# Starting the wide block's network inside its attention, and another order of the second experts' first steps

## Chip, cores and metric

The kernel runs on one core of a Trainium2 chip. The metric is the time of one execution in microseconds on the device, the median of several runs.

## What is computed

Four transformer blocks, each an attention and a network, on 1024 tokens (8 tiles of 128) of width 128. All is fp32. The change touches the second block, here called the wide block, and its experts:

```python
x = x + _L1_xattn_ref(_layernorm(x, axis=-1), ctx_1024, ...)
x = x + _L1_ffn_ref(_layernorm(x, axis=-1), ...)

# _L1_xattn_ref, 16 heads of width 128 and one score of a token with itself
x1 = _layernorm(attn_out + state_seq, g1, b1)
mlp = jax.nn.relu(x1 @ Wg + bg) * (x1 @ Wl + bl) @ Wm + bm      # width 512
return _layernorm(mlp + x1, g2, b2)

# _L1_ffn_ref, 16 experts of width 256, the best 2 of each token
logits = jnp.einsum('sbd,de->sbe', x, Wg) + bg + bias
vals, idx = jax.lax.top_k(logits, TOP_K)
w = jax.nn.softmax(vals - jnp.max(vals, axis=-1, keepdims=True), axis=-1)
cw = jnp.einsum('sbk,sbke->sbe', w, jax.nn.one_hot(idx, NUM_EXPERTS, dtype=x.dtype))
h = jax.nn.relu(jnp.einsum('sbd,edh->esbh', x, W1) + b1[:, None, None, :])
y = jnp.einsum('esbh,ehd->esbd', h, W2) + b2[:, None, None, :]
out = jnp.einsum('esbd,sbe->sbd', y, cw)
```

## The kernel before

Five engines each run one fixed list of instructions, in order, and meet at semaphores. Tokens are handled in two halves of 512. PSUM has 8 banks of 128x512. Products that need fp32 accuracy on the fast path are split in a high and a low part: `split_products` issues three 128x512 matmuls (low by high, high by low, high by high).

**Attention of the wide block.** `pipelined` writes out 32 steps (16 heads by 2 halves of tokens) of many stages. An entry `(stage, positions, lag)` runs the stage's unit n in step n + lag, in the order of the list. The stages `output` (lag 6) and `turn_sums` (lag 7) end it: the last heads' product is summed in bank 6, ScalarE copies it (`copy_sums`), TensorE turns it into bank 3, VectorE adds it to the tokens (`residual`, which counts `y_read`). The first half's norm is made in between (`statistics`, `variance`, `centre`, `scale`), so its tokens are turned in step 34 (`enter_mlp`), copied by ScalarE (`enter_halves`: the rounded `in_hi` and the full `xnT`) and their low part made by VectorE (`split_input(0)`).

**The wide block's network** (`ffn(mlp1)`). Per half: four slices `fc` of the hidden layer, each a gate product and an up product (3 matmuls each), ScalarE's relu, VectorE's `gate`, then `output`, 32 instructions of 128 columns. The second half's norm stands in VectorE's list ahead of the first gates (`mlp_norm(1)`). With 3 gate banks, slice 3 waits for the gate of slice 0 (`h_ready`).

**The experts** (`mixed(ffn1)`). 32 steps, each one expert and one half, in the list `order`; `hidden(s)` is 2 slices of 3 matmuls. The first 6 steps are *plain*: `plain_output` multiplies with fp32 weights and VectorE adds the result to the tokens by the routing weight `cw`. From step 6 on, VectorE scales the hidden layer itself by `cw_wide`, a row of routing weights spread over all partitions, and ScalarE and GpSimd split the result. `cw_wide` comes by a detour: TensorE turns `cw` (`turn_weights`), ScalarE copies it (`copy_weights`), SyncE stores it to DRAM (`cw_rows`) and loads two rows spread out (`load_wide`, 512 KB each). In TensorE's list of before: turn half 0, `hidden(0)`, turn half 1, `hidden(1)`, `routing`, `hidden(2)`, `plain_output(0)`, `hidden(3)`, `plain_output(1)`, `turn_weights`, `hidden(4)`, `plain_output(2)`, and so on.

**Weights.** An expert's first weights go through one staging buffer `w_in` (128 KB a load, `load_first`), the second ones through `w_out[e % 2]` (`load_second`). For experts 0 and 1 GpSimd makes both parts (`split_weights`); from expert 2 on ScalarE makes the high part (`round_first(e)`, which waits for the load) and GpSimd the low part (`split_first`), which then frees `w_in` for the next load. All loads are in SyncE's one list: `load_first(2)`, `load_first(3)`, `load_second(2)`, the store and two `load_wide`, `load_second(3)` (which waits for the second plain output of expert 1), `load_first(4)`, ... ScalarE's list has `router_exp` (the exponential that routing needs) at the start of step 2, `round_first(2)` after step 2, `round_first(3)` after step 3, then `copy_weights`, and `round_first(4)` after step 5.

`keep_busy(bank, n)` issues 2n matmul instructions of 128 columns with no use, so that TensorE is not idle. `inverse_roots` is GpSimd's part of a norm.

## Time and profile before

| | us |
|---|---|
| median of 3 runs | 779.91 (774.3 to 782.99) |
| the profiled execution's own time | 780.78 |
| its span, first to last instruction | 779.1 |
| TensorE busy | 723.9 (93%) |
| VectorE, ScalarE, GpSimd busy | 520.3, 458.7, 419.5 |
| mean granted TensorE clock, of full speed | 0.985 |

The wide block's attention lies at about 185 to 358 us, its network at 358 to 385, the experts' plain steps at 385 to 422. Matmuls are pipelined: a 128x512 one shows a duration of 0.39 us and starts 0.23 us after the one before.

### The profile page before, as it was taken

To read this page: it belongs to the slowest core of one execution; us is meant where nothing else is said; L and a number is where in the kernel's file an instruction comes from. 1 tells how busy PE (TensorE), PEld (TensorE's weight loads), DVE (VectorE), ACT (ScalarE), POOL (GpSimd) and SP (SyncE) were. 2 spreads that over 40 slices of the span, in tenths; PEclk is the share of its full clock that TensorE was granted. 3 is DMA by queue.
4 is the path that set the end of the run, shared out by engine and by line. 5 is a ranking of instruction groups with operands and counts; after the bars stand their busy time and mean duration, and the time that the engine had idled before them with its cause. 6 is when DMAs were issued, how large, how long until landed. Compare 5 with 4: busy or idle time off the path is not lost. (4 is left out here: it accounts for less than half of the span.)

```text
span 779.1 us, 14669 instructions
## 1 busy us (share of the span) xinstructions
PE 723.9 (93%) x5099; PEld 586.2 (75%) x5099; DVE 520.3 (67%) x1380; ACT 458.7 (59%) x1388; POOL 419.5 (54%) x414
## 2 busy tenths in 40 slices
PE   6989999998899999898979999989889999999896
PEld 3657987776788878776878788756668888888796
DVE  6888666676766666576756676658866466656666
ACT  3993556675877777563135676469924456656322
POOL 6875157774767543433223677466342378787311
PEclk9999999999999999899999999979999999999999
DMA  8004032210000000000003345000010232210000
GB/s 292 2 2 150 1 124 88 88 55 1 2 1 2 8 1 1 1 2 1 8 29 132 122 155 167 24 2 2 2 42 28 98 106 70 74 62 1 1 1 28
DMA packets 16361, 38.47 MB, mean 49 GB/s; under 512 B 1896, under 2 KB 6272, under 8 KB 16032
## 3 DMA queue, kind: packets, MB, share of 16 engines
q1 hardware_dynamic: 16288, 37.53, 14.3%
q8 instruction: 41, 0.67, 0.3%
q14 instruction: 32, 0.26, 0.1%
HBM read 36.87 MB, written 0.66 MB: 48 GB/s over the span
## 5 line engine op out<-in xcount | busy, mean ns | idle before, releaser
L1347 PE MATMUL banks<-input_hi,weights_in_lo 128*128 128x512 f32 x296 | 120.4, 407 | 5.2 <-PEq L1748 3.0
L1347 PE MATMUL banks<-input_lo,weights_in_hi 128*128 128x512 f32 x296 | 115.9, 391 | 0.0
L1347 PE MATMUL banks<-input_hi,weights_in_hi 128*128 128x512 f32 x296 | 115.7, 391 | 0.0
L1058 ACT ACTIVATE probabilities<-banks,neg_max 128x128 f32<-128x128 f32 x256 | 91.1, 470 | 12.6 <-DVE neg_max L2116 12.6
L877 POOL TENSOR_TENSOR hidden_lo<-hidden,hidden_hi 128x512 fp32r<-128x512 f32 x50 | 64.5, 1295 | 38.2 <-ACT hidden L1217 34.9
L725 POOL TENSOR_TENSOR rstd<-var_eps,neg_half 128x4 f32<-128x4 f32 x23 | 23.7, 1032 | 98.2 <-POOLq L724 78.6
L1058 ACT ACTIVATION_READ_ACCUMULATOR probabilities<-banks,neg_max 128x1 f32 x256 | 73.2, 311 | 0.0
L884 POOL TENSOR_TENSOR hidden<-hidden,scratch 128x512 f32<-128x512 f32 x48 | 62.1, 1293 | 19.7 <-ACT hidden L1203 17.2
L1347 PEld LDWEIGHTS banks<-input_hi,weights_in_lo 128*128 128x128 f32 x296 | 55.8, 189 | 19.6 <-issue 4.4
L1347 PE MATMUL banks<-hidden_hi,weights_out_lo 128*128 128x512 f32 x164 | 67.9, 414 | 1.5 <-POOL weights_out_lo L867 1.2
L1203 ACT ACTIVATE hidden<-banks 128x512 f32<-128x512 f32 x64 | 38.2, 598 | 51.8 <-PE banks L1347 51.6
L834 POOL TENSOR_TENSOR weights_in_lo<-weights_in,weights_in_hi 128x256 fp32r<-128x256 f32 (+2 forms) x31 | 40.1, 1293 | 52.6 <-ACT weights_in_hi L1228 51.7
L935 POOL TENSOR_TENSOR scratch<-values_state,self_weight 128x512 f32<-128x512 f32 x32 | 33.3, 1040 | 60.0 <-DVE self_weight L2275 60.0
L1347 PE MATMUL banks<-hidden_hi,weights_out_hi 128*128 128x512 f32 x164 | 65.2, 398 | 0.0
L1347 PEld LDWEIGHTS banks<-input_hi,weights_in_hi 128*128 128x128 f32 x296 | 55.6, 188 | 12.3
L1347 PEld LDWEIGHTS banks<-input_lo,weights_in_hi 128*128 128x128 f32 x296 | 55.9, 189 | 10.1
L1347 PE MATMUL banks<-weights_out,hidden 128*128 128x128 f32 x480 | 57.0, 276 | 2.5 <-PEq L1698 1.8
L1347 PEld LDWEIGHTS banks<-weights_out,hidden 128*128 128x128 f32 x480 | 55.7, 192 | 4.1 <-issue 2.3
L2464 DVE TENSOR_TENSOR banks<-banks,hidden 128x512 f32<-128x512 f32 x48 | 33.5, 698 | 33.1 <-POOL hidden L884 32.6
L2258 DVE TENSOR_REDUCE row_max<-banks 128x4 f32<-128x512 f32 x32 | 22.1, 691 | 47.1 <-PE banks L1593 47.1
L1347 PEld LDWEIGHTS banks<-identity 128*128 128x128 f32 x380 | 47.4, 197 | 7.3 <-issue 4.1
L1347 PE MATMUL banks<-identity 128*128 128x128 f32 x380 | 51.8, 284 | 1.0 <-DVE queries_feat L2070 1.0
(298 smaller groups left out, 1836.1 us busy)
## 6 DMA issues: line engine op xcount, KB each, us to landing
scratch<-cw_rows SPq DMA_DIRECT2D x25, 512.0 KB, 3.8
weights_out<-w_in SPq DMA_DIRECT2D x17, 256.0 KB, 2.8
weights_in<-w_in SPq DMA_DIRECT2D x8, 512.0 KB, 3.7
weights_in<-w_in SPq DMA_DIRECT2D x9, 256.0 KB, 2.7
weights_in<-w_in SPq DMA_DIRECT2D x16, 128.0 KB, 2.2
weights_out<-w_in SPq DMA_DIRECT2D x16, 128.0 KB, 2.1
wq<-w_in SPq DMA_DIRECT2D x1, 1024.0 KB, 5.2
wo<-w_in SPq DMA_DIRECT2D x1, 1024.0 KB, 7.4
```

Source lines behind the costliest of these rows:

```text
L725: pool.tensor_tensor(rstd[:, four], var_eps[:, four], neg_half[:, four], ALU.pow)\
L834: return pool.tensor_tensor(lo, raw, hi, ALU.subtract)
L877: pool.tensor_tensor(h_lo[:, j, :], h_full[:, j, :], h_hi32[:, j, :], ALU.subtract)\
L884: pool.tensor_tensor(h, h, cw_wide[:, e % 2, half * 512:(half + 1) * 512], ALU.mult)\
L935: pool.tensor_tensor(mva[:, n % 2, :, :], mv[:, four, :], self_w[:, n % 2, :, None].broadcast_to([P, 4, D]), ALU.mult)\
L1058: act.activation(prob[:, n // 2 % 2, h, :], b8(n % (2 if prune else 3))[:, i, :], ACT.Exp, bias=neg_max8[:, n % 4, i:i + 1], accum_out=z[: ...
L1203: act.activation(h_full[:, j, :], bank[f.hidden_bank(s, fc)][:, :], f.first, **kw)\
L1347: return pe.matmul(o, l, rh, start=start, stop=stop, **kw)
L2258: dve.tensor_reduce(m, b4(1 + n % 2), X_AX, ALU.max, negate=True).then_inc(st.sem, st.one())
L2464: dve.tensor_tensor(up, up, h, ALU.mult).then_inc(weighted_ready, 1)
```

## The change

Four things.

1. **Gates in the attention.** TensorE's gate products of slices 0 and 1, half 0, move from `ffn(mlp1)` into step 36 of the attention's list (`first_gates`), ahead of the last head's output. The up products get banks 5, 4, 3, so only slice 2 still waits for `y_read`. VectorE makes `split_input(0)` in step 35. The second half's norm is dealt out between the gates of the first half.
2. **Attention's first steps.** Turning the second half of the tokens, its copies and its keys and values (`turn_state`, `state_rest`, `take_tokens`, `evacuate_state_keys`, `state_values`) move one step later.
3. **Experts' order.** Steps 0 to 3 are now (expert 0, half 0), (1, 0), (0, 1), (1, 1). TensorE's list: turn half 0, filler, `hidden(0)`, `hidden(1)`, `plain_output(0)`, `plain_output(1)`, filler of 28 instructions, turn half 1, `routing`, small filler, `hidden(2)` to `hidden(5)`, `turn_weights`, `plain_output(2)`, `plain_output(3)`, and from `hidden(6)` on as before.
4. **Around it.** GpSimd splits expert 0's and expert 1's weights earlier in its list. ScalarE copies `xnT` ahead of `in_hi`; `router_exp` moves to the start of step 4, behind `round_first(3)`; `copy_weights` to step 5. SyncE's `load_second(2)` moves behind the two `load_wide`.

```diff
@@ class FFN
-                return 7 if self.gated and self.E == 1 else self.output_bank(half)
+                return 7 if self.gated and self.E == 1 else 4 + 3 * half if self.FC == 2 else self.output_bank(half)
+            def up_bank(self, fc):
+                return 5 - fc % 3
@@ class Experts
-                if gamma:
+                if gamma or self.FC == 2:
                     self.order[0:4] = [(0, 0), (1, 0), (0, 1), (1, 1)]
-                return (1, 0)
+                return (2, 0) if self.FC == 2 else (1, 0)
@@ SyncE, load_mixed
+                if f.gated:
                     load_second(2)
...
                 if f.gamma:
                     load_first(3)
+                if not f.gated:
                     load_second(2)
@@ GpSimd
-            inverse_roots((0, 0, 1))
+            inverse_roots((0,))
             split_weights(ffn1, 0)
-            inverse_roots((1,))
+            inverse_roots((0,))
+            split_weights(ffn1, 1)
+            inverse_roots((1, 1))
             mixed(ffn1)
@@ ScalarE, mixed
-                    if s == 2:
+                    if s == (4 if f.FC == 2 else 2):
                         router_exp()
...
                     if s in (2, 3):
                         round_first(s)
+                    if s == (5 if f.FC == 2 else f.turn_at):
+                        copy_weights()
                     if s == 5:
                         round_first(4)
-                    if s == f.turn_at:
-                        copy_weights()
@@ TensorE, wide_attention
+                def first_gates(it, n):
+                    pe.wait_ge(w_in_ready[0], 1)
+                    pe.sem_inc(w_in_ready[0], -1)
+                    pe.wait_ge(input_ready, 1)
+                    pe.sem_inc(input_ready, -1)
+                    mlp_gate(0, 0)
+                    mlp_gate(0, 1)
...
-                               (scores, range(32), 0), (state_rest, (0,), 1), (enter_mlp, (0,), 34)],
+                               (scores, range(32), 0), (state_rest, (0,), 2), (enter_mlp, (0,), 34),
+                               (first_gates, (0,), 36)],
@@ TensorE, ffn
-                                keep_busy(6, 5)
+                                keep_busy(6, 3)
                             pe.wait_ge(h_ready, 1)
...
-                            if half == 0 and fc == 0:
+                            if half == 0 and fc == 2:
                                 pe.wait_ge(y_read, 2)
@@ TensorE, mixed
-                    if s == 0 and not f.gated and not f.gamma:
+                    if s == 0 and f.FC == 2:
                         transpose_half(0, source, f.entry_bank(0))
-                    if s == 1 and not f.gamma:
-                        if not f.gated:
-                            keep_busy(6, 8)
+                        keep_busy(6, 12)
+                    if s == 2 and f.FC == 2:
+                        keep_busy(4, 14)
                         transpose_half(1, source, f.entry_bank(1))
-                    if s < 2 and not f.gamma:
-                        keep_busy(0 if f.gated and s == 0 else 6, ((16, 7), (3, 9))[f.gated][s])
+                        routing()
+                        keep_busy(0, 2)
...
-                    elif s == 1:
+                    elif s == 1 and f.gated:
                         routing()
...
-                    if f.lag <= s < f.lag + f.plain:
+                    if f.FC == 2 and s == 5:
+                        turn_weights()
+                    if f.FC == 2 and s < f.lag + 4:
+                        for step in {1: (0, 1), 5: (2, 3)}.get(s, ()):
+                            plain_output(step)
+                    elif f.lag <= s < f.lag + f.plain:
                         plain_output(s - f.lag)
...
-                    if s == f.turn_at and not f.gated and not f.gamma:
-                        turn_weights()
@@ VectorE, ffn
-                    for fc in range(f.FC):
-                        gate(0, fc)
+                    norm_stats(1, att, 1e-6)
+                    gate(0, 0)
+                    gate(0, 1)
+                    norm_apply(1, att, xm, norm_tok_ready, "g1", lambda b: row("be1"), lambda: gate(0, 2))
+                    dve.sem_inc(rows_wanted, 1)
+                    gate(0, 3)
                     split_input(1)
```

## Rows read from the trace of the kernel before

**Rows 1.** Waits of TensorE, 340 to 430 us.

```profile
PE banks L1358 <- PEq L1356: 2.0, 1, 2.0
```

**Rows 2.** Timeline of TensorE (start, length, instruction, [idle before]), attention's end.

```profile
356.26 0.50 PE L1347 MATMUL banks<-hidden_hi,hidden_lo 128*128 128x512 f32 x1 [0.72 <-DVE hidden_lo L2251]
...
357.92 0.66 PE L1644 MATMUL banks<-identity,scratch 128*128 128x128 f32 x4 [0.69 <-ACT scratch L1138]
...
366.80 1.06 PE L1347 MATMUL banks<-identity 128*128 128x128 f32 x8
...
368.53 3.70 PE L1347 MATMUL banks<-weights_out,hidden 128*128 128x128 f32 x31 [0.68 <-PEq L1698]
```

**Rows 3.** Timeline of VectorE, norms of the wide block.

```profile
378.37 1.13 DVE L2038 SCALAR_TENSOR_TENSOR x_tok<-values_state,rstd,x_tok 128x128 f32<-128x128 f32 x4
...
389.44 1.62 DVE L2038 SCALAR_TENSOR_TENSOR x_tok<-values_state,rstd,x_tok 128x128 f32<-128x128 f32 x4 [0.17 <-DVEq L2035]
```

**Rows 4.** Timeline of GpSimd: splitting expert 0's first weights.

```profile
389.40 0.72 POOL L834 TENSOR_TENSOR weights_in_lo<-weights_in,weights_in_hi 128x256 fp32r<-128x256 f32 x1
```

**Rows 5.** Timeline of TensorE, the experts' first steps.

```profile
385.00 3.74 PE L1347 MATMUL banks<-identity 128*128 128x128 f32 x32
...
390.47 0.47 PE L1347 MATMUL banks<-input_hi,weights_in_lo 128*128 128x512 f32 x1 [1.73 <-PEq L1748]
...
391.92 1.95 PE L1347 MATMUL banks<-identity 128*128 128x128 f32 x16
...
400.19 1.85 PE L1347 MATMUL banks<-square_weights,xn_feat 128*128 128x16 f32 x16
...
408.87 1.03 PE L1794 MATMUL banks<-identity,combine_weights 128*16 128x128 f32 x8 [0.41 <-PEq L1789]
...
423.65 0.50 PE L1347 MATMUL banks<-input_hi,weights_in_lo 128*128 128x512 f32 x1 [0.36 <-DVE hidden_lo L2481]
```

**Rows 6.** Timeline of ScalarE, experts' first steps; last row from block 0.

```profile
399.70 1.38 ACT L1203 ACTIVATE hidden<-banks,cols 128x512 f32<-128x512 f32 x2 [2.00 <-PE banks L1347]
...
404.37 0.21 ACT L1164 ACTIVATE gap_exp<-gap 128x8 f32<-128x8 f32 x1 [3.30 <-ACTq L1163]
...
405.63 0.41 ACT L1228 ACTIVATE weights_in_hi<-weights_in 128x256 fp32r<-128x256 f32 x1
...
409.36 0.42 ACT L1228 ACTIVATE weights_in_hi<-weights_in 128x256 fp32r<-128x256 f32 x1 [1.96 <-ACTq L1222]
...
420.48 0.42 ACT L1228 ACTIVATE weights_in_hi<-weights_in 128x256 fp32r<-128x256 f32 x1 [5.23 <-ACTq L1222]
...
106.44 0.72 ACT L1225 ACTIVATE weights_in_hi<-weights_in,cols 128x512 fp32r<-128x512 f32 x1 [5.54 <-ACTq L1222]
```

**Rows 7.** Timeline of VectorE, routing.

```profile
404.02 0.17 DVE L2353 TENSOR_TENSOR gap<-best 128x8 f32<-128x8 f32 x1
...
408.22 0.29 DVE L2382 TENSOR_TENSOR combine_weights<-combine_weights,combine_weights_second 128x128 f32<-128x128 f32 x1
```

**Rows 8.** Timeline of the DMA queue (start of issue); last two rows from block 0.

```profile
412.74 0.80 SPq L631 DMA_DIRECT2D scratch<-cw_rows  x2
...
416.76 0.33 SPq L612 DMA_DIRECT2D weights_in<-w_in  x1
...
100.50 0.80 SPq L631 DMA_DIRECT2D scratch<-cw_rows  x2
...
101.41 0.36 SPq L612 DMA_DIRECT2D weights_in<-w_in  x1
```

**Rows 9.** Timeline of TensorE: its two longest waits.

```profile
316.57 0.65 PE L1347 MATMUL banks<-scratch,ones 128*32 128x128 f32 x8 [2.88 <-POOL scratch L927]
...
577.75 0.63 PE L1358 MATMUL banks<-identity,xn_tok 128*128 128x128 f32 x4 [2.42 <-PEq L1356]
```

**Rows 10.** Windows of 4 us; the granted clock is third from the end.

```profile
316.00:320.00 4.00, 3.43 (x18) 2.68 (x19) 0.88 (x6) 1.16 (x3) 2.74 (x3) 0.50 0.01 4
...
320.00:324.00 4.00, 4.00 (x23) 3.77 (x22) 3.48 (x13) 1.82 (x9) 0.30 (x1) 0.65 0.00 0
```

More of the change, by code:

```diff
@@ L885, in scale @@
                         .then_inc(scaled_ready, 1)
-                if not f.gamma:
+                if f.gated:
                     split_weights(f, 1)
@@ L1027, in take @@
                     source = bank[f.entry_bank(half)][:, :]
+                    act.activation(xnT[:, tokens], source, ACT.Copy).then_inc(feat_ready, 1)
                     act.activation(in_hi[:, 0, tokens], source, ACT.Copy).then_inc(st.sem, st.one())
-                    act.activation(xnT[:, tokens], source, ACT.Copy).then_inc(st.sem, st.one())
                     act.wait_ge(st.sem, st.n)
                     act.sem_inc(input_hi_ready, 1)
-                    act.sem_inc(feat_ready, 1)
                 if not begun:
@@ L1100, in evacuate_state_keys @@
                 act.wait_ge(projected_act, half + 3)
-                act.activation(qT[:, half * 512:(half + 1) * 512], bank[2 + half][:, :], ACT.Identity,
+                act.activation(qT[:, half * 512:(half + 1) * 512], bank[2 + 4 * half][:, :], ACT.Identity,
                                bias=col("bk1")).then_inc(keys_ready, 1)
@@ L1151, in enter_mlp @@
                     enter_halves(mlp1)
-                pipelined(act, [(take_tokens, (1,), 0), (enter_mlp, (0,), 35),
+                pipelined(act, [(enter_mlp, (0,), 35),
                                 (copy_probsT, range(32), 3), (exps, range(32), 2), (copy_own, range(32), 1),
-                                (queries, range(32), 0), (evacuate_state_keys, (1,), 0),
+                                (queries, range(32), 0), (take_tokens, (1,), 0), (evacuate_state_keys, (1,), 1),
                                 (lambda it, n: round_heads(wo1, wo_hi, 0), (2,), 0),
@@ L1575, in state_rest @@
                     pe.sem_inc(feat_ready, -1)
[L1576 removed]
+                    project(w("wk1"), xnT, 5, (1,), projected_act)
                     project_tok(w("wv1"), xnT, 4, (0,))
@@ L1649, in enter_mlp, with mlp_gate @@
                     transpose_half(0, iv, mlp1.entry_bank(0))
-                pipelined(pe, [(queries, range(32), 0), (turn_state, (0,), 0), (own_sums, range(32), 1),
+                def first_gates(it, n):
[5 more added lines that the diff above has]
+                    mlp_gate(0, 1)
+                pipelined(pe, [(queries, range(32), 0), (turn_state, (0,), 1), (own_sums, range(32), 1),
                                (output, range(32), 6), (turn_heads, range(32), 4), (turn_own, range(32), 1),
                                (values, range(32), 3), (turn_sums, (15, 31), 7), (turn, range(32), 2),
-                               (scores, range(32), 0), (state_rest, (0,), 1), (enter_mlp, (0,), 34)],
+                               (scores, range(32), 0), (state_rest, (0,), 2), (enter_mlp, (0,), 34),
+                               (first_gates, (0,), 36)],
                           32, 1, lambda: None)
+            def mlp_gate(half, fc):
+                tokens = slice(half * 512, (half + 1) * 512)
+                return split_products(bank[mlp1.hidden_bank(half, fc)][:, :],
+                                      lambda part: mlp1.w1((w_lo, w_hi)[part], 0, fc),
+                                      lambda part: (in_lo, in_hi)[part][:, 0, tokens], True, True)
             def route(weight, experts, src, at=7):
@@ L1663, in hidden @@
                 def hidden(half):
-                    if half == 0:
+                    if half == 0 and not f.gated:
                         pe.wait_ge(w_in_ready[0], 1)
                         pe.sem_inc(w_in_ready[0], -1)
-                    pe.wait_ge(input_ready, 1)
-                    pe.sem_inc(input_ready, -1)
+                    if half == 1 or not f.gated:
+                        pe.wait_ge(input_ready, 1)
+                        pe.sem_inc(input_ready, -1)
                     tokens = slice(half * 512, (half + 1) * 512)
@@ L1674, in hidden @@
                             if half == 0:
-                                keep_busy(6, 5)
+                                keep_busy(6, 3)
                             pe.wait_ge(h_ready, 1)
                         at_bank = f.hidden_bank(half, fc)
-                        m = split_products(bank[at_bank][:, :],
-                                           lambda part: f.w1((w_lo, w_hi)[part], 0, fc),
-                                           lambda part: (in_lo, in_hi)[part][:, 0, tokens], True, True)
+                        if not f.gated or half == 1 or fc >= 2:
+                            m = split_products(bank[at_bank][:, :],
+                                               lambda part: f.w1((w_lo, w_hi)[part], 0, fc),
+                                               lambda part: (in_lo, in_hi)[part][:, 0, tokens], True, True)
                         if f.gated:
-                            if half == 0 and fc == 0:
+                            if half == 0 and fc == 2:
                                 pe.wait_ge(y_read, 2)
-                            m = split_products(bank[3 + at_bank][:, :],
+                            m = split_products(bank[f.up_bank(fc)][:, :],
                                                lambda part: f.up((w_lo, w_hi)[part], 0, fc),
@@ L2232, in narrow_attention @@
                                     (copy_both, range(UNITS), 2), (first_output, (0,), 15)], UNITS, 1, st.close)
-            def mlp_norm(half, *args):
-                norm_half(half, att, xm, 1e-6, norm_tok_ready, "g1", lambda b: row("be1"), *args)
             def wide_attention():
@@ L2328, in wide_attention @@
                 st.close()
-                pipelined(dve, [(heads_out, range(32), 4), (weights, range(32), 3), (state_values, (0,), 2),
+                pipelined(dve, [(heads_out, range(32), 4), (weights, range(32), 3), (state_values, (0,), 3),
+                                (lambda it, n: split_input(0), (0,), 35),
                                 (maxima, range(32), 1), (low_headsT, range(32), 4), (second_tokens, (0,), 2),
                                 (residual, (15, 31), 7),
-                                (lambda it, n: split_input(0), (0,), 37),
                                 (statistics, (0, 2), 23), (variance, (0,), 26), (centre, (0, 2), 27),
@@ L2407, in gate @@
                     dve.sem_inc(g_done, -1)
-                    h, up = hT[:, half, fc, :], bank[3 + f.hidden_bank(half, fc)][:, :]
+                    h, up = hT[:, half, fc, :], bank[f.up_bank(fc)][:, :]
                     dve.scalar_tensor_tensor(h, up, col(f.up_bias, fc), h, ALU.add, ALU.mult)\
```

7 lines of the change are left out of this document (4 added, 3 removed).

## The prediction

> **What bounds the kernel now.** I read the page first: TensorE is busy 93% of the span and no other engine over 67%, so time can come only out of TensorE's waits, fillers and half-speed stretches. Between the attention's last head and step 8 of the experts the timeline shows which. Before the network's first output product stand a wait of 0.72 for the last head's low part, one of 0.69 for ScalarE's copy, a filler of 1.06 and a wait of 0.68 [rows 2]. Before the experts stand a filler of 3.74, a wait of 1.73, a filler of 1.95 [rows 5] and a wait of 2.0 for the tokens of half 1 [rows 1]. The next thing to read is what TensorE meets behind that stretch: step 8 waits 0.36 at 423.65 [rows 5], released by VectorE's low part, which follows ScalarE's rounding, and ScalarE had stood still 5.23 until the first weights of expert 4 were there, at 420.48 [rows 6]. That load had been issued at 416.76 [rows 8]. So the plain steps are bound twice, by TensorE and, almost level with it, by a chain: turned routing weights, their trip through DRAM, the load of expert 4, ScalarE, VectorE, TensorE. A gain ahead of step 8 counts only as far as this chain comes earlier too.
>
> **Part 1, the attention's start.** Turning half 1 one step later lets the first scores go about 0.9 earlier, and the state's projections then stand behind step 2. ScalarE's list (a rounding of weights, a copy, the exponentials) sets the third step as before. I take a gain of 0.4; bounds 0.9 and a loss of 0.3, since the projections need about 2.7 wherever they stand.
>
> **Part 2, gates in the attention.** Six matmuls of 0.23 each take the place of the wait of 0.72 [rows 2]: the last head's product starts at 356.75 instead of 356.26, the turned sums at 358.41 instead of 357.92. From there the two up products (1.4) and slice 2 (1.4) end at 361.8. VectorE: residual to 359.8, statistics of half 1 to 361.5, two gates of 0.7 to 363.0, centring 1.1, third gate 0.7, scaling 1.1: tokens of half 1 at 366.4. Slice 3 ends at 363.95 on TensorE, which then waits 2.4 for these tokens, where before it had them. The turning (0.45) and the filler of 8 (0.95) end at 367.9; the fourth gate is done at 367.2. The first output product starts at 367.9 against 368.53 [rows 2]: a gain of 0.6. The rows that GpSimd adds (two of 2.4 after 366.4, done at 371.2) are still ahead of VectorE's need of them at 371.9.
>
> **Part 3, the split of expert 0's weights.** It was the last thing that the wait until 390.47 was for: GpSimd ended it at 390.12 [rows 4, 5]. It moves to about 378, beside VectorE's norm of half 0. What that costs is shown by the same norm instruction, 1.13 for four alone and 1.62 beside this split [rows 3]; a loss of 0 to 0.5, which may eat the 0.6 above. I take 0.3. The Trainium skill (SBUF — State Buffer, Who interferes with whom) says that a VectorE instruction with two SBUF inputs and a reading GpSimd instruction exclude each other for a whole instruction. By it the first of the four would wait up to 1.0, the length of GpSimd's rounding, and nothing would be left of the gain; the row shows half of that.
>
> **Part 4, the experts' first steps.** Output products, 0.3 earlier, end at 384.2; turning and 24 fillers (2.8 at the rate of 3.74 for 32 [rows 5]) end at 387.5. VectorE has half 0's low part at 387.8, so `hidden(0)` starts there, 2.7 ahead of before. Expert 1's first weights: their load stands in SyncE's list behind `load_second(0)`, which waits for the network's last output of half 0 to be read (384.5); landing 2.2 later, split 1.9, so 389.1. `hidden(1)` starts at 389.3. Two plain outputs of 1.7 end at 394.1 and 28 fillers (3.3) at 397.4. GpSimd's root for half 1 now stands behind the split and comes about 1.5 later; the tokens of half 1 are there at 395.7, under that filler. Turning and ScalarE's copy take 1.4, 0.9 of it waiting; routing 1.7; filler 0.5: `hidden(2)` starts at about 401.0 (400.2 to 401.3). Before it was 401.9 (400.19 plus 16 pieces [rows 5]). From here on I count from this start, H.
>
> TensorE's four hidden steps end at H+5.6, and the next entry turns the routing weights. When are they ready? ScalarE ends step 2 at H+2.4 and rounds expert 2; round_first(3) needs GpSimd's split and a load, and started 3.73 after round_first(2) before (405.63 to 409.36 [rows 6]), hence H+6.1. `router_exp` now stands behind it: exponential ready at H+6.7. Before it ran 0.35 after its input (404.02, 404.37 [rows 6, 7]). Routing needs 2.75 more behind it (405.76 to the row at 408.22 and its end, 408.51 [rows 7]), and 0.36 to reach TensorE: turning starts at H+9.75. TensorE waits 4.1, which was 0.41 before [rows 5]. This is the wait that takes the place of those removed. Two plain outputs follow, the first held by VectorE's sum to H+10.9, the second ends at H+14.3. For `hidden(6)` that is 415.3, against 416.0.
>
> The chain: copies end 1.6 after the turning started, the store takes 2.0 (410.76 to 412.74), so the two wide loads are issued at H+13.4 against H+10.85 before [rows 8]. Behind them stand now three loads of 128 KB, the last, expert 4's, at H+15.1; before it was H+14.9. The nearest case in the trace is block 0: wide loads issued at 100.50, 256 KB right behind them, there at 106.4, 5.9 later [rows 6, 8]. With 0.13 MB more at some 270 GB/s I take 6.3: H+19.7, that is 420.7. Bounds: 5.8 (nothing for the larger volume) and 7.7 (before, from the wide issue at 412.74 to 420.48 [rows 6, 8]). Before, ScalarE had it at 420.4. From there to TensorE's wait it takes the same 3.2: 423.9 against 423.65. So everything gained ahead of step 8 is waited away there: a loss of 0.25, less the 0.4 of part 1. The Trainium skill (DMA: Bandwidth & Descriptors, Anatomy of one DMA) gives about 2.0 us a transfer plus its bytes at 436 GB/s. By that estimate the queue of 1.4 MB would be in 5.3 after the first issue, and the sum 1.0 lower; block 0 shows 5.9 for less.
>
> **The clock.** Two waits of TensorE in this trace reach 2.4 (2.88 and 2.42 [rows 9]). After the first, with TensorE busy throughout ahead of it, the granted clock was 0.50 and then 0.65 over 8 us [rows 10], the lower level of 1.2 GHz; the work from 316.57 to 323.3 took 6.7 where other steps show 3.9. The waits of 1.73 and 2.0 inside our stretch left it at full speed. The wait of 4.1 is beyond both, so I count a fall there: turning and two plain outputs at half speed end 2 later, half of it hidden, since TensorE would wait at step 8 anyway; the loads behind them come 0.6 to 1.1 later. I take 1.0.
>
> **Sum.** 780.78 (this execution's own time) - 0.4 + 0.25 + 1.0 = 781.6. The median shown is 0.9 below this execution, so I forecast 781.0, 1.1 above the median: no change that can be measured. A measurement of this kernel tells about 1%, 7.8 us, from no change; the three runs before lie 8.7 apart.
>
> **Rivals.**
> - *The clock falls at the gates too (slower).* TensorE idles 2.4 at 364 to 366.4, as long as the 2.42 of the trace that was followed by a fall. Low for 3.4 to 6.8 us, it would run filler and output product at half speed, and these lie on the path: 1.5 to 3. With the fall at the routing: 783.5. It decides from the length at which idle time costs the clock; between 2.0 (no fall) and 2.42 (a fall) the trace doesn't say, and a wait of 1.93 elsewhere, among sparse work, had one too.
> - *The late router isn't late (faster).* If the load of expert 3 or the exponential were there in time, turning would start at H+5.9, the wide loads at H+9.5, expert 4's at H+11, and step 8 would be reached about 3 earlier, with no fall: 776.5. Against it: ScalarE's list is in order, and 3.73 between the two roundings is measured.
> - *The clock holds at the routing.* Then the sum is 780.6, or 780.0 against the median; this differs from the forecast by less than the runs do.
> - *The reorder moves later stretches.* The falls at 316 and 577 need not come at the same places when all work before them is shifted; one more or one less is 3 either way.
>
> **Chances.** Forecast 0.40, both falls 0.25, clock holds 0.20, router in time 0.10, others 0.05. The range from 776 to 786 takes in the router in time, both falls with their upper bound of 3 and one fall elsewhere. Faster by over 1% 0.03, within 1% 0.91, slower by over 1% 0.06.
>
> **What would show it.** In the changed trace: two gate products of three ahead of the last head's output, and a wait of about 2.4 before half 1 of the network's tokens is turned; no wait for weights before `hidden(0)`; the exponential of routing directly behind the rounding of expert 3; a wait of about 4 before the routing weights are turned, a granted clock under 1 behind it; ScalarE waiting for expert 4's weights until 20 after `hidden(2)` began; and the steady steps from step 8 on within 1 of their place. The forecast is wrong if TensorE reaches step 8 early and finds the low part there, if TensorE's routing wait is short, or if the clock changes outside the stretch.

## The result, and the profile after

| | before | after |
|---|---|---|
| median of 20 runs, us | 779.89 (774.3 to 782.99) | 783.52 (776.87 to 787.16) |
| ratio, 95% interval | | 1.0057 (1.0037 to 1.0076) |
| profiled execution's own time, its span | 780.78, 779.1 | 786.86, 785.1 |
| mean granted clock | 0.985 | 0.979 |

The changed kernel is 0.6% slower (779.89 x 0.0057 = 4.4 by the ratio, 3.6 by the medians), which is inside the 1% that I called no change. Its profiled execution is 3.3 above its own median and before's 0.9 above its own, so of the 6.0 between the spans about 2.4 belong to the executions and not to the kernels.

The waits of TensorE, 340 to 430 us; columns: waiting line, releaser, us in total, times, longest:

```profile
PE banks L1353 <- PEq L1830: 3.2, 1, 3.2
PE banks L1821 <- PEq L1816: 3.0, 1, 3.0
...
PE banks L1364 <- PEq L1362: 2.2, 1, 2.2
```

Before, the longest wait of this stretch was 2.0 [rows 1]; now three reach 2.2 to 3.2. TensorE's timeline at the attention's end (start, length, instruction, [idle before]):

```profile
357.26 0.66 PE L1650 MATMUL banks<-identity,scratch 128*128 128x128 f32 x4 [0.69 <-ACT scratch L1144]
...
365.19 0.63 PE L1364 MATMUL banks<-identity,values_ctx 128*128 128x128 f32 x4 [2.17 <-PEq L1362]
365.65 1.56 PE L1353 MATMUL banks<-identity 128*128 128x128 f32 x8
367.01 4.90 PE L1353 MATMUL banks<-weights_out,hidden 128*128 128x128 f32 x32
```

The turned sums came at 357.92 and the output product at 368.53 [rows 2], so the product starts 1.5 earlier. But half 1's tokens are waited for 2.17, and the product, 3.70 long for 31 instructions before, takes 4.90 for 32 (3.74 in E2 below, at full clock). TensorE in the experts' first steps:

```profile
388.25 0.47 PE L1353 MATMUL banks<-input_hi,weights_in_lo 128*128 128x512 f32 x1 [0.33 <-PEq L1775]
...
399.48 1.93 PE L1353 MATMUL banks<-square_weights,xn_feat 128*128 128x16 f32 x16 [0.86 <-PEq L1809]
...
401.70 0.48 PE L1353 MATMUL banks<-input_hi,weights_in_lo 128*128 128x512 f32 x1
...
405.36 0.47 PE L1353 MATMUL banks<-input_hi,weights_in_lo 128*128 128x512 f32 x1 [0.65 <-PEq L1772]
...
411.34 1.87 PE L1821 MATMUL banks<-identity,combine_weights 128*16 128x128 f32 x8 [2.99 <-PEq L1816]
413.00 5.76 PE L1353 MATMUL banks<-weights_out,hidden 128*128 128x128 f32 x32
...
423.31 3.06 PE L1353 MATMUL banks<-weights_out,hidden 128*128 128x128 f32 x16 [3.18 <-PEq L1830]
...
430.66 0.39 PE L1353 MATMUL banks<-input_hi,weights_in_lo 128*128 128x512 f32 x1
```

The gain is still there at 388.25 (2.2 ahead of 390.47 [rows 5]). At 399.48 the routing is only 0.7 ahead of 400.19, but two plain outputs (391.31 to 394.88, 3.57), which stood behind it before, are done by then. So up to here the new order is some 4 ahead, and the loss lies all behind `hidden(2)`, which starts at 401.70. Turning the routing weights is 2.5 late against 408.87, after a wait of 2.99. At 423.31 the first output of expert 2 waits 3.18, and step 8's second slice is reached 7.0 after its time in [rows 5]. The releaser L1830 is TensorE's own sequencer; that line stands right behind `pe.wait_ge(w_out_loaded[sub], 16)`, the wait for the second weights. Who had those, by SyncE's queue (start of issue):

```profile
413.85 0.33 SPq L648 DMA_DIRECT2D cw_rows<-att_feat  x1
417.18 0.80 SPq L634 DMA_DIRECT2D scratch<-cw_rows  x2
418.03 1.09 SPq L625 DMA_DIRECT2D weights_out<-w_in  x2
419.27 0.33 SPq L615 DMA_DIRECT2D weights_in<-w_in  x1
```

At 417.18 the two wide loads, at 418.03 two loads of second weights (expert 2's and expert 3's), at 419.27 expert 4's first weights. Before, the wide loads went out at 412.74 and expert 4's at 416.76 [rows 8], and expert 2's second weights had been loaded ahead of the store. ScalarE:

```profile
407.66 0.42 ACT L1234 ACTIVATE weights_in_hi<-weights_in 128x256 fp32r<-128x256 f32 x1 [2.14 <-ACTq L1228]
407.98 0.19 ACT L1170 ACTIVATE gap_exp<-gap 128x8 f32<-128x8 f32 x1
...
423.82 0.42 ACT L1234 ACTIVATE weights_in_hi<-weights_in 128x256 fp32r<-128x256 f32 x1 [9.99 <-ACTq L1228]
```

The exponential stands directly behind the rounding of expert 3, 3.6 later than the 404.37 of [rows 6], and expert 4's weights are rounded at 423.82 instead of 420.48. VectorE's norm of half 0, beside which GpSimd now splits expert 0's weights, and the granted clock (third from the end) in windows of 4 us:

```profile
377.95 1.60 DVE L2068 SCALAR_TENSOR_TENSOR x_tok<-values_state,rstd,x_tok 128x128 f32<-128x128 f32 x4
```

```profile
316.00:320.00 4.00, 4.00 (x19) 3.51 (x16) 1.07 (x4) 1.45 (x3) 2.19 (x2) 0.50 0.02 4
...
364.00:368.00 4.00, 2.81 (x17) 2.84 (x18) 2.52 (x6) 1.09 (x2) 2.68 (x2) 0.76 0.00 0
...
368.00:372.00 4.00, 4.00 (x31) 3.96 (x30) 0.22 (x1) 0.00 (x0) 3.32 (x2) 0.82 0.00 0
...
412.00:416.00 4.00, 4.00 (x21) 3.69 (x20) 1.38 (x5) 1.17 (x2) 0.00 (x0) 0.50 0.12 19
...
416.00:420.00 4.00, 4.00 (x25) 3.54 (x24) 2.25 (x8) 0.00 (x0) 0.00 (x0) 0.84 0.48 100
...
424.00:428.00 4.00, 4.00 (x18) 3.62 (x18) 1.34 (x5) 2.17 (x5) 2.69 (x3) 0.57 0.02 4
```

The clock fell to its lower level of 1.2 GHz behind each of the three waits: in parts of 364 to 372, from the turning at 411.34 to 420, and in 424 to 428. The first row answers to [rows 10]: the fall after the wait of 2.88 in the attention is there as before.

### The profile page after: what moved, and what is told of

It is laid out like the page before. It is cut to its first block and busy times, and to the rows that moved or that the text cites. A ratio compares the mean times of both kernels' runs of the same rounds, so it can differ in the third digit from the quotient of the medians.

```text
span 785.1 us, 14642 instructions
## 1 busy us (share of the span) xinstructions
PE 726.8 (93%) x5089; PEld 588.8 (75%) x5089; DVE 518.6 (66%) x1380; ACT 458.2 (58%) x1388; POOL 419.5 (53%) x414
## 5 line engine op out<-in xcount | busy, mean ns | idle before, releaser
L1353 PE MATMUL banks<-weights_out,hidden 128*128 128x128 f32 x480 | 60.9, 288 | 5.5 <-PEq L1830 3.2
L1353 PEld LDWEIGHTS banks<-weights_out,hidden 128*128 128x128 f32 x480 | 59.6, 204 | 7.1 <-issue 5.5
```

Of the source, the lines that this page charges most:

```text
L1353: return pe.matmul(o, l, rh, start=start, stop=stop, **kw)
```

## The experiments

Each time is a median of 12 runs (9 of E12, 6 of E11), beside runs of the kernel before, which were 779.28 for E1 to E4, 779.90 for E5 to E8 and 778.81 for E9 to E12. Since each profile is one execution, I also read from each trace how long TensorE takes between fixed points: from the turned sums (357.92 before) to the first split output product of step 6 (425.59 before), 67.67 in the kernel before and 75.22 in the changed one. "Stretch" below is this difference.

**E1 and E2, the parts without the experts.** E1 is the kernel before with only the attention's first steps changed; E2 is the changed kernel with the experts' part of the diff put back (ScalarE's new order of its copies stays). Core of E1's edit; the copies, keys and values of half 1 move one step in the same way:

```diff
-                pipelined(pe, [(queries, range(32), 0), (turn_state, (0,), 0), (own_sums, range(32), 1),
+                pipelined(pe, [(queries, range(32), 0), (turn_state, (0,), 1), (own_sums, range(32), 1),
...
-                               (scores, range(32), 0), (state_rest, (0,), 1), (enter_mlp, (0,), 34)],
+                               (scores, range(32), 0), (state_rest, (0,), 2), (enter_mlp, (0,), 34)],
```

> The kernel before with the attention's first steps of the change alone (turning and projecting half 1 one step later). Theory A (the loss of the change lies in the experts' order, in two new waits of TensorE of 3.0 and 3.2 us and the half-speed stretches behind them; the attention's start is a gain): the queries at 312 us come 1.1 earlier, as they do in the changed kernel, and the time is 1 below before, ratio 0.998 to 1.000. Theory B (work that is shifted gains or loses falls of the clock elsewhere, and that is what the medians show): the stretch is 1.1 shorter but the median moves by up to 3 us either way.

> The changed kernel with the experts' order, routing, loads and GpSimd's list put back: what is left is the attention's start and the gates in the attention. Theory A: TensorE waits 2.2 for half 1's tokens of the network and the clock falls behind it in most executions; net of the 1.1 of the attention's start and 0.5 of the gates, less 1.3 for the clock, 0 to 2 us faster than before, ratio 0.997 to 1.000. Rival C (the gates are the loss, since a wait of 2.2 and half speed stand on the path that was covered before): 2 us or more slower, ratio over 1.002.

Measured: E1 776.98, ratio 0.9971 (0.9944 to 0.9998); E2 776.44, ratio 0.9977 (0.9955 to 0.9999). Rival C is out: without the experts' part nothing is lost. Both theories on E1 hold in part, for it gained 2.3 by the medians and only 1.1 of it is seen in what was changed. The size of part 1 is read best between block 0's last output product and a head some steps on. Before, after, E1:

```profile
178.74 1.13 PE L1347 MATMUL banks<-hidden_lo,weights_out_hi 128*128 128x512 f32 x4
...
204.50 0.43 PE L1347 MATMUL banks<-scratch,ones 128*32 128x128 f32 x8 [0.72 <-POOL scratch L927]
```

```profile
178.78 1.12 PE L1353 MATMUL banks<-hidden_lo,weights_out_hi 128*128 128x512 f32 x4
...
203.44 0.43 PE L1353 MATMUL banks<-scratch,ones 128*32 128x128 f32 x8
```

```profile
179.79 0.89 PE L1347 MATMUL banks<-hidden_lo,weights_out_hi 128*128 128x512 f32 x3
...
204.46 0.43 PE L1347 MATMUL banks<-scratch,ones 128*32 128x128 f32 x8
```

The row of 178.74 groups four instructions, E1's one at 179.79 starts the same group. That is 25.76 before, 24.66 after, 24.67 in E1: part 1 gains 1.1. E1's execution happened to reach block 0's end 1.0 later and so starts its heads level with before, yet it ends 4.4 earlier, and 2.9 of that are there at the turned sums (354.99 against 357.92). Where from? After the same wait of 2.88 in the attention (at 316.53) its clock did not fall:

```profile
316.00:320.00 4.00, 3.47 (x32) 3.13 (x33) 2.25 (x9) 1.70 (x4) 2.69 (x3) 1.00 0.01 4
```

The fall was there in eight of the eleven profiles that have this wait (before, after, E3, E4, E5, E6, E8, E9) and absent in E1, E2 and E7. From this wait to the turned sums TensorE took 38.5 to 38.9 without the fall and 39.8 to 41.7 with it: 1 to 3 us that a kernel pays or not by execution. E2's stretch is 65.93, 1.7 shorter than before, with a wait of 2.2 before half 1 is turned and no fall behind it: in that trace, with the clock up, the gates are a gain. The medians don't show it, for E2 is 0.5 below E1 and its ratio 0.0006 above E1's.

**E3, the experts' order alone.** The kernel before with parts 3 and 4 of the change.

> The kernel before with the experts' order, routing, loads and GpSimd's list of the change, and without the attention's start and the gates. Theory A: a wait of 3 before the routing weights are turned and one of 3 before the first plain output of expert 2 are there as in the changed kernel, the loss is at least that of the whole change: 4 to 6 us slower, ratio 1.005 to 1.008. Rival C: no slower than before, ratio under 1.002.

Measured: 783.34, ratio 1.0067 (1.004 to 1.0094), as theory A had it; stretch 71.71, 4.0 longer than before. The whole loss of the change is in this part. Its two waits:

```profile
410.94 1.14 PE L1801 MATMUL banks<-identity,combine_weights 128*16 128x128 f32 x8 [2.90 <-PEq L1796]
...
420.55 2.02 PE L1350 MATMUL banks<-weights_out,hidden 128*128 128x128 f32 x16 [1.81 <-PEq L1810]
```

The second wait is shorter here, and the clock stayed up behind it (2.02 for the output). TensorE came to it later: the clock had fallen already between 400 and 404 (granted 0.69), though the longest wait since 388 was 0.86.

**E4, the router's exponential earlier.** The changed kernel with one move in ScalarE's list:

```diff
-                    if s == (4 if f.FC == 2 else 2):
+                    if s == 2 and f.FC != 2:
                         router_exp()
...
+                    if s == 3 and f.FC == 2:
+                        router_exp()
                     if s in (2, 3):
                         round_first(s)
```

> The changed kernel with ScalarE's exponential of routing ahead of the rounding of expert 3's weights instead of behind it. Theory A: the exponential starts 2.5 earlier, TensorE's wait before the turned routing weights goes from 3.0 to about 0.5 and no fall of the clock stands behind it; the wide loads and all behind them start 3 to 4 earlier, since the fall had stretched the copies too; the wait for expert 2's second weights stays (3 or more, for TensorE now comes earlier). 2 to 4 us under the changed kernel, about level with before: ratio 0.999 to 1.003. Rival D (the wait for expert 2's weights takes over whatever is gained ahead of it, as they sit behind the wide loads, whose start depends on the cw turning alone): the loads come earlier by the same amount, so the wait does not grow; if it grew to 6, the time would stay at 1.006.

Measured: 781.35, ratio 1.0038 (1.0013 to 1.0064). The exponential starts at 405.08, 2.9 earlier. TensorE:

```profile
408.04 1.03 PE L1823 MATMUL banks<-identity,combine_weights 128*16 128x128 f32 x8
...
419.20 3.51 PE L1355 MATMUL banks<-weights_out,hidden 128*128 128x128 f32 x16 [4.84 <-PEq L1832]
```

The first wait and its fall are gone, and the second grew from 3.18 to 4.84, with a fall behind it. So the two waits are not one: the second ends 6.3 after the wide loads are issued (412.92 here), whenever TensorE comes. A gain ahead of it counts as far as it brings the wide loads earlier, and no further. Here they are issued 4.0 earlier, counted from the turned sums, and the stretch is 3.8 shorter, 71.44. The median is 2.2 below the changed kernel's; the ratio, 1.0038 against 1.0057, doesn't tell them apart.

**E5, expert 2's second weights ahead of the wide loads.** The changed kernel with:

```diff
                 sp.dma_start(f.cw_rows, cwT[0:f.E, :]).then_inc(cw_stored, 16)
+                if f.FC == 2:
+                    load_second(2)
                 sp.wait_ge(cw_stored, 16)
...
-                if not f.gated:
+                if f.gamma:
                     load_second(2)
```

> The changed kernel with expert 2's second weights loaded between the store of the routing weights and the two wide loads, instead of behind these. Theory A (two separate waits, each followed by half speed): the wait of 3.2 before the first plain output of expert 2 is gone, the wait of 3.0 before the routing weights are turned stays with its fall; 3 to 5 us under the changed kernel, ratio to before 0.999 to 1.002. Theory E (the chain through expert 4's first weights would bind step 8 anyway, as the prediction said): the wait moves to step 8, and only 0 to 2 us are gained, ratio 1.003 to 1.006.

Measured: 781.64, ratio 1.0014 (0.9994 to 1.0033); stretch 70.24. Theory A has the ratio right, theory E the new wait at step 8 and the size of the gain. TensorE:

```profile
410.19 1.03 PE L1823 MATMUL banks<-identity,combine_weights 128*16 128x128 f32 x8 [2.98 <-PEq L1818]
411.31 5.43 PE L1355 MATMUL banks<-weights_out,hidden 128*128 128x128 f32 x32
...
417.98 1.95 PE L1355 MATMUL banks<-weights_out,hidden 128*128 128x128 f32 x16
...
424.52 0.50 PE L1355 MATMUL banks<-input_hi,weights_in_lo 128*128 128x512 f32 x1 [0.73 <-DVE hidden_lo L2514]
```

The wait of 3.18 is gone; the wait of 2.98 at the turning and the half speed behind it (5.43 for two outputs) stay; and now the wait at step 8 is back, 0.73 at 424.52, for VectorE's low part as in [rows 5]. The load of the second weights had to wait for its buffer, which the outputs of expert 0 free: it was issued at 414.74, 2.8 behind the store, and held the wide loads back to 415.18. The median is 1.9 below the changed kernel's, though the two were measured beside different runs of before.

**E6, both edits.**

> The changed kernel with both edits: the exponential of routing ahead of the rounding of expert 3, and expert 2's second weights ahead of the wide loads. Theory A: neither wait is left; turning at 408, expert 2's output without a wait at 414, step 8 at 420 to 422 against 423.65 before and 430.7 in the changed kernel; 5 to 8 us under the changed kernel, ratio to before 0.995 to 0.998, level with the attention's part alone or 1 below it. Theory E: step 8 waits for expert 4's weights, there at 419 to 420, and is no earlier than 422.3: the experts' order then gives nothing over the attention's part alone (0.997 to 0.998).

Measured: 779.17, ratio 0.9977 (0.9952 to 1.0002); stretch 67.09. TensorE:

```profile
408.18 1.03 PE L1825 MATMUL banks<-identity,combine_weights 128*16 128x128 f32 x8
...
420.47 0.47 PE L1357 MATMUL banks<-input_hi,weights_in_lo 128*128 128x512 f32 x1 [1.00 <-DVE hidden L2505]
...
422.22 0.50 PE L1357 MATMUL banks<-input_hi,weights_in_lo 128*128 128x512 f32 x1 [0.82 <-DVE hidden_lo L2516]
```

ScalarE:

```profile
419.05 0.42 ACT L1236 ACTIVATE weights_in_hi<-weights_in 128x256 fp32r<-128x256 f32 x1 [7.95 <-ACTq L1230]
```

Neither wait is left. In their place the two slices of step 8 wait 1.00 and 0.82 for VectorE, behind ScalarE, behind expert 4's weights. From their rounding to the second slice it is 3.17 (419.05 to 422.22), as in E5, in E7 and in the kernel before (420.48 to 423.65 [rows 5, 6]). That is the chain which the prediction named; mending everything ahead of it brings the kernel only back to it, as theory E said.

**E7 and E8, filler.** E7 is E6 with filler ahead of the turning of half 1; E8 is the changed kernel with this filler and another ahead of the routing weights, and both waits left as they are.

```diff
                 hidden(0)
+                if f.gated:
+                    keep_busy(6, 8)
                 transpose_half(1, source, f.entry_bank(1))
...
                     if f.FC == 2 and s == 5:
+                        keep_busy(7, 12)
                         turn_weights()
```

> The same with 16 filler instructions (1.9 us) in TensorE's wait of 2.2 before half 1's tokens of the network are turned. Theory A: no fall of the clock behind that wait in any profile; half speed there had cost 1.3 in the changed kernel's trace, and it falls in some executions only, so the median is 0.5 to 1.3 lower than without the filler. Rival: the fall comes by chance at other waits as well and the medians do not differ by more than 0.5.

> The changed kernel with fillers only: 16 instructions in the wait of 2.2 at the gates, 24 (2.8 us) in the wait of 3.0 before the routing weights are turned; no wait is taken away. Theory A: the granted clock stays at 1.00 behind both, which gives back 1.3 at the gates and about 2.4 at the two plain outputs; the wide loads come about 1 earlier, and the wait for expert 2's second weights takes up part of the rest: 1.5 to 3.5 us under the changed kernel, ratio to before 1.001 to 1.004. If half speed costs nothing there because TensorE waits later anyway: no difference from the changed kernel, 1.005 to 1.006.

Measured: E7 777.33, ratio 0.997 (0.9948 to 0.9992), stretch 65.54; E8 782.81, ratio 1.0033 (1.0009 to 1.0057), stretch 74.44. In E7 the tokens wait 0.39 and the output product runs at full speed; from the turned sums it starts 9.30 later, against 10.61 before and 9.75 after. E7's median is 1.8 below E6's (0.5 by the ratios), E8's 0.7 below the changed kernel's, less than the runs can tell. In E8 no clock falls at the gates nor at the turning, and the two outputs take 3.81 instead of 5.76. But the fifth output comes only 1.9 earlier, counted from the turned sums, as the wide loads do, and the clock fell in two other places of the stretch. One is in 396 to 404 (granted 0.83, 0.74), with no wait above 0.86 since 386. The other is behind the second wait.

```profile
411.43 3.81 PE L1353 MATMUL banks<-weights_out,hidden 128*128 128x128 f32 x32
...
420.13 3.75 PE L1353 MATMUL banks<-weights_out,hidden 128*128 128x128 f32 x16 [3.50 <-PEq L1832]
```

The wait is 3.50, and the output behind it takes 3.75, where it is 1.95 at full clock.

**E9, the missed wait in the kernel before.** Only `load_second(2)` moves behind the two `load_wide`.

> The kernel before, with one edit: SyncE's load of expert 2's second weights stands behind the two wide loads instead of ahead of the store. Theory A (these weights bind the fifth plain output): in the kernel before the wide loads are issued at 412.74 and the fifth plain output starts at 417.47; the new place of the load lets it land 5.2 to 6 after the wide loads, at 418 to 418.8, so TensorE waits 0.5 to 1.3 there, without a fall of the clock; the wait of 0.36 at step 8 goes, expert 4's load lands up to 0.5 later: in all 0 to +1, median 779.5 to 781. In the changed kernel the same place costs 3 and more only because the router's wait had already pushed the wide loads later. Theory B (the load's place costs by itself, wherever the router stands): a wait of over 2 and a fall, +3, median 783.

Measured: 779.34 beside 778.81, ratio 1.001 (0.999 to 1.003).

```profile
412.06 0.80 SPq L631 DMA_DIRECT2D scratch<-cw_rows  x2
...
418.19 2.02 PE L1349 MATMUL banks<-weights_out,hidden 128*128 128x128 f32 x16 [1.22 <-PEq L1805]
```

The output waits 1.22, ready 6.1 after the wide loads are issued, as in the changed kernel (417.18 to 423.31). With the router in time this costs 0.5, inside what the runs can tell; theory A held. Its stretch, 69.31, is 1.6 longer than before. Part of that is an earlier wait of the stretch, 1.99 for half 1's tokens at 394.37, which had a fall of the clock behind it, as it hadn't in the trace of before. The place of the load becomes dear when the wide loads are late.

**E10, E11 and E12, towards a faster kernel.** GpSimd's list in the attention holds the root of a norm ahead of a product that TensorE needs. The kernel before:

```profile
313.16 1.04 POOL L725 TENSOR_TENSOR rstd<-var_eps,neg_half 128x4 f32<-128x4 f32 x1 [6.27 <-POOLq L724]
...
315.17 1.26 POOL L927 TENSOR_TENSOR scratch<-scratch,queries_feat 128x512 f32<-128x512 f32 x1
```

GpSimd stood 6.27 for the root's input, and TensorE 2.88 for the product behind it [rows 9]. The edit is one number:

```diff
-                pipelined(pool, [(lambda it, n: inverse_roots((0,)), (15,), 12), (self_values, range(32), 4),
+                pipelined(pool, [(lambda it, n: inverse_roots((0,)), (15,), 13), (self_values, range(32), 4),
```

E10 is the kernel before with it; E11 is E2 with it and E7's filler; E12 is E7 with it.

> The kernel before, with one edit in the wide block's attention: GpSimd's root of the norm of half 0 stands one step later in its list (lag 13 instead of 12), behind that step's product of values. The wait of 2.88 at 316.57 was for GpSimd, which had stood idle 6.27 waiting for the input of that root with the product behind it. Theory A: the wait goes, and with it the fall of the clock that follows in some executions: 2.5 to 2.9 less in every run and up to 3 more in some, median 774 to 777. Rival: the attention's later steps wait for VectorE or ScalarE instead, so that only the fall goes: 0 to -2, median 778 to 780; or the later root holds up the norm and the turning of the tokens at the attention's end: +1.

> The changed kernel with the experts' part put back (attention's first steps and gates only), plus 16 filler instructions ahead of turning half 1 at the gates, plus GpSimd's root one step later. From 776.4 for the first two parts alone: the root gives -2.5 to -3, the filler keeps the clock at the gates: median 771 to 774. If the root's wait is absorbed by another engine: 775 to 777.

> The changed kernel with the routing exponential one step earlier, expert 2's second weights ahead of the wide loads, filler at the gates, and GpSimd's root one step later in the attention. From 777.3 without the root: 773 to 775 if the root's wait goes, 776 to 778 if another wait takes its place. Whether the experts' new order, both waits mended, is worth anything: it should come out within 1 of the kernel with the old order, the filler and the root; if the order saves its 2 of filler in full, it is 2 faster than that.

Measured: E10 774.94, ratio 0.9964 (0.9942 to 0.9987); E11 772.57, ratio 0.9925 (0.99 to 0.995); E12 773.77, ratio 0.994 (0.9919 to 0.996), each in its expected range. E10, GpSimd and TensorE:

```profile
314.23 1.04 POOL L725 TENSOR_TENSOR rstd<-var_eps,neg_half 128x4 f32<-128x4 f32 x1 [1.15 <-POOLq L724]
```

```profile
314.69 0.43 PE L1347 MATMUL banks<-scratch,ones 128*32 128x128 f32 x8
```

The wait is gone and so is the fall. E11, with attention, gates, filler and root and the experts' old order, beats both kernels: 6.2 below the 778.81 of before by the medians. E12, with the new order mended, is 1.2 above it in the median, its interval overlapping, and 2.1 below it in the profiled spans (770.2 and 772.3). So whether the mended order is worth anything stays open within 2 us. In the traces the best stretch with the new order is 65.54 (E7) and with the old one 65.93 (E2), one execution each: 0.4.

## Why the prediction was right or wrong

The median, 783.52, lies in the range and within 1% of before. It is 2.5 above my 781.0, and the steps that made it are only in part mine: that it came so near is in part luck.

- **Part 1** was mis-sized: -0.4 forecast, -1.1 measured, beyond my bound of -0.9.
- **Part 2** held. The new products move the turned sums by 0.40, forecast 0.49: 38.46 from the wait of 2.88 to them in E1 and 38.86 in E2, both at full clock, and 45.17 and 45.57 from the query ahead of it (312.75, 311.69) in the two kernels, both with a fall. Half 1's tokens are there 7.93 after the turned sums, forecast 8.0, though the terms that I listed for them add up to 365.9 and not 366.4. The wait for them is 2.17, forecast 2.4. With the clock up, the output product starts 9.30 after the turned sums (E2, E7, E8), forecast 9.5.
- **The fall at the gates**, my slower rival, was there in the changed kernel, E4, E5 and E6, and absent in E2. Its price was 1.2 in the output product and 0.5 in the filler, 1.7. Of these 1.36 reach the network's second output product (23.52 from the turned sums to 380.78; 22.16 in E7), just under my 1.5 to 3. I gave both falls together 0.25; four profiles of five showed this one. I had it decided by the length of the wait, and that failed: 2.17 was followed by a fall in four profiles and not in E2.
- **Part 3** held: the norm took 1.60 beside the split, as it had 1.62 beside it before [rows 3], and E2 has 1.13 there, without the split. TensorE's wait for the second half's output in the network grew from 0.89 to 1.41 in E3, which has the split and not the gates. By my estimate from the Trainium skill's rule (SBUF — State Buffer, Who interferes with whom), that the two engines lock each other out, it would have been up to 1.0; the trace shows 0.5.
- **Routing** held. `hidden(2)` began at H = 401.70 (forecast 401.0), the exponential stood behind expert 3's rounding, turning began at H+9.64 (forecast H+9.75), the clock fell behind it and the two outputs took 2.0 more, the turning 0.8. The wait was 2.99, not 4.1, because TensorE had reached it 1.1 later after H than forecast; 0.65 of that is a wait of `hidden(4)` for expert 2's first weights (405.36), which I had not counted. The wide loads went out at H+15.5, where I had H+13.4 and 0.6 to 1.1 for the clock: the copies ended 2.5 after the turning began instead of 1.6, and the loads followed the store by 3.3 instead of 2.0.
- **The step that failed** is part 4's "Two plain outputs follow ... for `hidden(6)` that is 415.3" together with "The chain": I listed the three loads behind the wide ones and priced the last of them, expert 4's. The first of them, expert 2's second weights, is needed by the fifth plain output, which comes ahead of step 8. Its moving was in the diff and in my text of the change. My own numbers had the wait in them: `hidden(6)` from H+14.3 ends at H+15.7, and the load, 5.9 behind wide loads at H+13.4 as in block 0 [rows 6, 8], is there at H+19.3. That is 3.6 waited, and 5.8 more to step 8's second slice (417.47 to 423.65 before, less the wait of 0.36) give H+25.1, 2.2 past my 22.9. Measured, it costs a wait of 3.18, a fall behind it, and whatever is gained ahead of it without bringing the wide loads earlier (E8). From H to step 8's second slice I had 22.9 and 1.0 for the clock; it took 28.96.
- **The chain through expert 4's load** was rightly built: rounded 6.6 after the wide loads were issued (6.3 forecast; 5.9 to 6.8 in E3 to E9), and binding as soon as the missed wait is mended (E5, E6). In the changed kernel as it is, it does not bind.
- **The sum** came out near because errors cancelled: part 1 gained 0.7 more, the chain did not bind, the missed wait and the two further falls cost more. The parts by medians are -2.84 (E2) and +4.06 (E3), together +1.2, where 3.6 was measured; by the ratios they are -1.8 and +5.2, together +3.4, where 4.4 was measured. The intervals of the two parts reach 2 us to either side each, so no run shows that the parts do more together than apart.
- **"Router in time, 776.5"** was mis-built: with the router in time (E4) the kernel stood at 781.35, for the second weights held it.
- **The clock behind short waits.** I read from one trace that the wait of 2.0 leaves the clock up. In other executions it doesn't (last section). The wait that I gave as 1.93 is 1.92 in the trace, at 509.89; its fall is there in every profile but E5's.

## What to carry to other kernels

When a queue's entry is moved, ask of every entry that it moves behind, and of the moved one itself, which instruction waits for it first, and price each; the last one in the queue isn't always the one that binds. A wait whose end is set by another engine's chain takes back what is gained ahead of it, unless the gain brings that chain earlier too: with the load unmoved, the fillers of E8 gave 0.8 of stretch, the earlier router of E4, which starts the chain, 3.8. When an order is moved, compare two traces where the same work is done, not where the same instruction stands: at the routing the changed kernel looked 0.7 ahead and was some 4. And look for an engine that stands idle at an instruction whose input is late with a ready one behind it: that one number in GpSimd's list gained 0.4% by itself (E10), where the whole change lost 0.6%.

## What I had not expected of the hardware

The same wait, 2.88 in the same place of the same instructions, was followed by a lower clock in eight executions and not in three, and the wait of 2.17 or 2.18 before half 1 is turned in four of five. The experts' old order has a wait of 1.98 to 2.00 before half 1 is turned. The clock stayed up behind it in the kernel before and in E2, and fell in E1, E9, E10 and E11. The filler behind it in the kernel before, then this wait and filler in E1, where the windows of 392 to 400 have 0.66 and 0.91:

```profile
396.32 1.73 PE L1347 MATMUL banks<-identity 128*128 128x128 f32 x14
```

```profile
392.97 0.77 PE L1358 MATMUL banks<-identity,xn_tok 128*128 128x128 f32 x4 [1.98 <-PEq L1356]
393.53 3.20 PE L1347 MATMUL banks<-identity 128*128 128x128 f32 x14
```

E3 and E8 had a fall at the routing behind no wait above 0.86. So the length of a wait does not by itself decide, and a single profile can differ by 1 to 3 us from another of the same kernel for this reason. The Trainium skill (TensorE: Matmul & The Clock Gate, Part 1: The HAM clock gate) says that the chip's watch over TensorE's activity runs free of the kernel; these rows agree with that. The spread of 10 us in the 20 runs of the changed kernel goes with the clock: the two fastest (776.87, 777.28) have a mean granted clock of 0.991, the two slowest (787.0, 787.16) 0.981 and 0.978. What makes it differ from run to run, no run shows. Filler of 16 instructions that left 0.39 of the 2.17 kept the clock up at the gates in all four profiles that had it (E7, E8, E11, E12).

The first load behind the two wide ones was ready for use at a steady time after the wide loads' issue: 5.9 to 6.3 us in E3, E4, E8, E9 and the changed kernel. The two wide loads went out 2.0 after the store in most traces and 3.3 after it in the changed kernel's (413.85 and 417.18), with no load between them as in E5; why, no run here shows.
